# A graph attention layer on one core: the head and the second round of the pipeline put in another order

## The chip, the core and the metric

The kernel runs on one core of a Trainium2 chip. The metric is the device time of one execution in microseconds (us). Five engines run their own instruction streams beside each other and wait for one another by semaphores: PE (matrix products), DVE and ACT (vector and scalar work), POOL (vector work, slower) and SP (which only issues DMAs here).

## What is computed

There are 128 graphs of 64 nodes with 384 features each; `adj` (128 x 64 x 64) is 0 or 1 here. With every bias random and small:

```python
h = jnp.maximum(_layernorm(x, axis=-1), 0.0)
adj = dep_type_matrix != 0
dep_emb = dep_emb_table[dep_type_matrix]
hi_t = einsum('bid,de->bie', h, W1_w[:HID])[:, :, None, :] + einsum('bijd,de->bije', dep_emb, W1_w[HID:]) + W1_b
hj_t = einsum('bjd,de->bje', h, W2_w[:HID])[:, None, :, :] + einsum('bijd,de->bije', dep_emb, W2_w[HID:]) + W2_b
relevance = jnp.sum(hi_t * hj_t, axis=-1)
A = softmax(where(adj, relevance, NEG), axis=2)
h_syn = relu(einsum('bij,bjd->bid', A, h) @ gcn_w + gcn_b)
x = x + h_syn @ Wo_w + Wo_b
```

Where an edge exists its type is 1, so the type's part of both factors is one vector each: q (from W2) and p (from W1), each the embedding row times the 64 lower rows of the weight, plus its bias. Relevance is then h M h' plus a term by row, a term by column and a constant, with M = W1 W2' (384 x 384). The kernel tests at run time whether a type above 1 occurs (`has_types`) and jumps over a slower branch when, as here, none does.

## The kernel before

**Tiles.** A supertile is 8 graphs, 512 rows of x, in KT = 4 tiles of 128 rows; there are 16 supertiles. h stands transposed in hT, in DC = 3 chunks of 128 features. Products keep fp32 accuracy by splitting each operand in a high and a low fp16 part (`..._hi`, `..._lo`) and adding three fp16 products; those are the lines L1142 to L1144 whatever the product is (`split_product`).

**A supertile's work on PE**, in five kinds: `g_chunk` (G = M h, three chunks of 9 matmuls with 512 columns), `hg_tile` (h times gcn_w, four tiles of 9 matmuls with 385 columns, the 385th is the row term), `transposed_attention` and `aggregation` (attention times h gcn_w), `scores_of` (h' G, 48 short matmuls) and `output` (four tiles of 9 matmuls with 384 columns). ACT takes the high part of every result out of its bank (`g_high_part`, `hg_high_part`, `z_parts`), DVE the low part (`g_low_part`, `hg_low` inside `rows_and_low`, `z_low_part`), and both of them do the softmax between them: `masked_scores` and the maximum on DVE, `move_scores` and `exponentials` on ACT, `attention` on DVE.

**The order** is written out by hand, one list for each engine; semaphores tie the lists together. Supertiles 0 and 1 are handled apart from the rest. First comes a head: W1 and W2 are transposed on PE (L1163) and copied to SBUF, M is made in three chunks (L1183), p and q are projected (L1202), a bound on M's size fixes M's power-of-two scale (`scale`, by `peak_exponent`, `scale_from_exponent`, `scale_ready`), the norms of gcn_w and Wo fix theirs, x(0) is normalised (`first_coefficients`, `early_normalise`) and its h is transposed on PE (L1175) rather than by DMA. Then the first round (`g_chunk` and `hg_tile` of supertile 0), the jump on `has_types` (L256), the transposes of h(1), the scores of 0, and the second round: supertile 1 with attention and output of 0. From supertile 2 on h is transposed by DMA, and the loop has two supertiles in each pass.

**POOL** adds the output bias to x (`add_bias`, L408), turns adj from int to the score bias (`make_bias`, L402, two halves), works out the layer norm coefficients of later supertiles (`coefficients`, L345, 20 short instructions) and takes the low part of h (L432). **SP** issues the loads, `transpose_h` and the stores.

The 8 banks of PSUM are handed from product to product: `FIRST_HG_BANK` gives the banks of the four hg tiles of supertile 0, `EARLY_BANK` those of the transposes of h.

Of the kernel before, what the change touches and what calls it, by code (L numbers as in the profile page):

```python
# [5 lines left out]
def gnn_layer_program(nc, x, adj, emb, W1, b1, W2, b2, gcn_w, gcn_b, Wo, bo, out):  # L6
# [50 lines left out]
    with ctx:  # L57
# [136 lines left out]
        EARLY_BANK = (3, 4, 5)  # L194
        FIRST_HG_BANK = (3, 4, 5, 0)
        WARM_UP = 10
        EARLY_WIDE = 2
# [8 lines left out]
        early_bank = [bank[b][:, :].rearrange("p (k t) -> p k t", k=KT) for b in EARLY_BANK]  # L206
# [53 lines left out]
        def _(sp):  # L260
# [64 lines left out]
        def _(pool):  # L325
# [53 lines left out]
            def main_coefficients(s):  # L379

                pool.wait_ge(stats_ready, s + 1)

                if isinstance(s, int) and s <= 3:
                    pool.wait_ge(coef_ready, COEF_STEPS * s)
                    pool.wait_ge(h_ready, 2 * KT * min(s, 2))
                else:
                    pool.wait_ge(h_ready, 2 * KT * s)
                coefficients(s, third_stats6 if isinstance(s, int) and s == 2 else stats6, *normal_terms(s), coef_ready)

            pool.dma_start(bo_all[:, 0, :], bo.partition_broadcast(P)).then_inc(bo_loaded, 16)  # L390
# [52 lines left out]
            token_low(2, range(0, HALF_TILES))  # L443
            token_low(2, range(HALF_TILES, KT))
# [9 lines left out]
        def _(act):  # L454
# [39 lines left out]
            def early_high_part(s, c):  # L494
                act.wait_ge(early_t, DC * s + c + 1)
                nc.scalar.activation(hT_parts[s][:, :, 0, c, :], early_bank[c], ACT.Relu).then_inc(early_high, 1)
# [77 lines left out]
            early_high_part(0, 1)  # L574
            early_high_part(0, 2)
# [12 lines left out]
            types_above(2)  # L588
            g_high_part(0, 2)
            g_whole(2)  # L590
            hg_high_part(0, 0)
            types_above(3)
            hg_high_part(0, 1)
            early_normalise(1, range(0, EARLY_WIDE))
# [20 lines left out]
            def move_scores(s):  # L615
                act.wait_ge(s_done, s + 1)
                for g in range(GT):
# [24 lines left out]
            def second_round():  # L642
                for c in range(DC):
                    early_high_part(1, c)
                for c in range(DC):
                    wo_high_part(c)
                move_scores(0)
                g_high_part(1, 0)
                g_whole(0)
                exponentials(0)  # L650
                g_high_part(1, 1)
                g_whole(1)
                third_tokens(range(0, HALF_TILES))
                attention_out(1)
                g_high_part(1, 2)
                g_whole(2)
                third_tokens(range(HALF_TILES, KT))
                aggregated(1)
# [29 lines left out]
        def _(dve):  # L688
# [26 lines left out]
            def early_low_part(s, c):  # L715
                dve.wait_ge(early_high, DC * s + c + 1)
                nc.vector.scalar_tensor_tensor(hT_parts[s][:, :, 1, c, :], early_bank[c], 0.0, hT_parts[s][:, :, 0, c, :],
# [6 lines left out]
            def first_coefficients():  # L724
# [7 lines left out]
                dve.wait_ge(q_copied, 2)  # L732
                nc.vector.tensor_reduce(pq_size[:, :], pq_cols[:, :].unsqueeze(2), AX.X, ALU.max,
                                        apply_absolute_value=True).then_inc(top_step, 1)
                dve.wait_ge(coef_step, 1)
                nc.vector.scalar_tensor_tensor(sq, gap, D / 4, gap, ALU.mult, ALU.mult).then_inc(coef_step, 1)
                dve.wait_ge(top_step, 3)
                nc.vector.tensor_tensor(pq_size[:, :], pq_size[:, :], w_top[:, :, :].rearrange("p n c -> p (n c)"),
                                        ALU.max).then_inc(top_step, 1)
                dve.wait_ge(coef_step, 4)  # L740
                nc.vector.scalar_tensor_tensor(var, sq, D * EPS, var, ALU.add, ALU.add).then_inc(coef_step, 1)
                dve.wait_ge(top_step, 4)
                nc.vector.tensor_tensor(w_bound[:, :], pq_size[:, 0:DC], pq_size[:, DC:2 * DC],
                                        ALU.mult).then_inc(top_step, 1)
# [3 lines left out]
                dve.wait_ge(top_step, 5)  # L748
                nc.vector.tensor_reduce(bound_sum[:, :], w_bound[:, :], AX.X, ALU.add).then_inc(bound_ready, 1)
# [9 lines left out]
                def refine(n):  # L759
# [4 lines left out]
                times_var(0)  # L764
                refine(0)
                square(1)
                times_var(1)
                refine(1)
                square(2)
                dve.wait_ge(bound_wide, 1)  # L770
                nc.vector.tensor_scalar(peak[:, SC_M:SC_M + 1], pq_bank[:, BOUND, 0:1], TINY, None,
                                        ALU.max).then_inc(scale_step, 1)
                times_var(2)
                peak_exponent(SC_M, SC_M + 1, 1)
                refine(2)
                scale_from_exponent(SC_M, SC_M + 1, 1)
                dve.wait_ge(coef_step, 15)
                nc.vector.tensor_scalar(ln_mul, root, H_SCALE * D ** 0.5, None, ALU.mult).then_inc(coef_step, 1)
                scale_ready(SC_M, SC_M + 1, 1, m_scale_ready)
                dve.wait_ge(coef_step, 16)  # L780
                nc.vector.scalar_tensor_tensor(ln_add, total, -0.5, ln_mul, ALU.mult, ALU.mult)\
                  .then_inc(coef_ready, COEF_STEPS)
# [718 lines left out]
```

## Time and profile before

| | us |
|---|---|
| median of 3 runs | 365.49 (364.24 to 365.90) |
| the profiled execution's own time | 364.34 |
| its span | 362.4 |
| around the span | 1.94 |
| PE busy | 350.7, 97% of the span |
| ACT busy | 271.6, 75% |
| DVE busy | 262.4, 72% |
| POOL busy | 172.8, 48% |

The span runs from the first to the last instruction of the profiled execution, and every start below is counted from its beginning. TensorE's granted clock was full throughout. A matmul's end is modelled: in a row of back-to-back matmuls with 385 columns each shows 0.33 us, though they start 0.16 us apart. An idle time in brackets is counted from the modelled end, so the next matmul's start moved by 0.16 us more than the bracket says.

### The profile page before, as it was taken

What the parts mean: (1) busy time and instruction counts of PE and PEld (TensorE: products, weight loads), DVE (VectorE), ACT (ScalarE), POOL (GpSimd) and SP (SyncE); (2) the same over time, 40 slices, a digit from 0 to 9 for tenths busy, and PEclk for the clock granted to TensorE, in tenths of its full rate; (3) what the DMA queues carried; (4) which work ended last, traced back from release to release, by engine and by line L of the source; (5) the groups of instructions that cost most, each with busy time, mean ns of one, the idle gap of its engine ahead of it and who ended that gap; (6) DMA issues with size and microseconds to landing.
All of it is one profiled execution on the core that took longest, in us unless ns stands there. A gap on an engine that the chain in (4) does not pass through costs nothing.

```text
span 362.4 us, 9435 instructions
## 1 busy us (share of the span) xinstructions
PE 350.7 (97%) x3124; PEld 217.7 (60%) x3124; DVE 262.4 (72%) x668; ACT 271.6 (75%) x577; POOL 172.8 (48%) x349
## 2 busy tenths in 40 slices
PE   7998879999999999999999999999999999999986
PEld 7764546565756566565756666565756656565753
DVE  0998698594968767695867767695867768576664
ACT  3398795978698877778698877778788777765732
POOL 2056735655627183745728183744718174670000
DMA  7993608955547393655548393655648363544053
GB/s 220 325 251 90 175 5 140 225 132 153 145 134 207 87 260 88 196 110 151 151 127 221 87 258 89 185 114 142 167 113 234 87 174 87 117 92 143 2 143 121
DMA packets 82215, 53.87 MB, mean 149 GB/s; under 512 B 45666, under 2 KB 82148, under 8 KB 82196
## 3 DMA queue, kind: packets, MB, share of 16 engines
q1 hardware_dynamic: 81488, 53.22, 56.6%
q0 software_dynamic: 64, 0.20, 0.3%
q10 hardware_dynamic: 644, 0.20, 0.2%
q8 instruction: 11, 0.18, 0.2%
q14 instruction: 8, 0.07, 0.1%
HBM read 17.44 MB, written 12.58 MB: 83 GB/s over the span
## 4 chain that ended last, share of the span: by engine, by line
PE 85%; DVE 7%; ACT 2%; DMA 2%; POOL 2%; issue 2%; DVEq 0%; SPq 0%; ACTq 0%; POOLq 0%
PE bank L1142 24%; PE bank L1143 23%; PE bank L1144 23%; PE bank L1242 3%; PE bank L1393 3%; PE bank L1388 3%; PE bank L1250 2%; DMA x_all<-in_L_gnn_W_w_dram 2%; DVE stats L711 1%; PE bank L1359 1%; ACT h_tok L491 1%; PE bank L1175 1%; POOL root_sq L345 1%; PE bank L1458 1%; PE bank L1460 1%
## 5 line engine op out<-in xcount | busy, mean ns | idle before, releaser
L432 POOL TENSOR_TENSOR h_parts<-h_tok,h_parts 128x1536 f16<-128x1536 f32 (+1 forms) x15 | 43.8, 2922 | 101.2 <-ACT h_parts L473 93.6
L1142 PE MATMUL bank<-gw_hi,hT 128*128 128x385 f16 x192 | 63.0, 328 | 2.2 <-DVE hg_lo L812 2.2
L1144 PE MATMUL bank<-gw_hi,hT 128*128 128x385 f16 x192 | 62.7, 327 | 0.0
L408 POOL TENSOR_TENSOR x_all<-x_all,bo_all 128x1536 f32 (+1 forms) x16 | 54.9, 3439 | 16.0 <-ACT h_tok L491 16.0
L1143 PE MATMUL bank<-gw_lo,hT 128*128 128x385 f16 x192 | 62.5, 326 | 0.0
L1142 PE MATMUL bank<-wo_hi,z_hi 128*128 128x384 f16 x180 | 58.8, 327 | 0.0
L1143 PE MATMUL bank<-wo_lo,z_hi 128*128 128x384 f16 x180 | 58.7, 326 | 0.0
L1144 PE MATMUL bank<-wo_hi,z_lo 128*128 128x384 f16 x180 | 58.7, 326 | 0.0
L1142 PE MATMUL bank<-hT,m_hi 128*128 128x512 f16 x144 | 54.6, 379 | 0.0
L1143 PE MATMUL bank<-hT,m_hi 128*128 128x512 f16 x144 | 54.6, 379 | 0.0
L1144 PE MATMUL bank<-hT,m_lo 128*128 128x512 f16 x144 | 54.6, 379 | 0.0
L895 DVE TENSOR_TENSOR g_parts<-bank,g_parts 128x512 f16<-128x512 f32 x48 | 33.2, 691 | 28.3 <-ACT bank L546 27.9
L541 ACT ACTIVATE g_parts<-bank,pair_bias 128x512 f16<-128x512 f32 x48 | 32.9, 685 | 18.3 <-PE bank L1144 18.3
L553 ACT ACTIVATE z_hi<-bank,gcn_bias 128x512 f16<-128x512 f32 x48 | 33.8, 704 | 12.0 <-PE bank L1393 12.0
L1018 DVE TENSOR_TENSOR z_lo<-bank,z_hi 128x512 f16<-128x512 f32 x48 | 32.9, 685 | 8.5 <-ACT bank L555 8.4
L560 ACT ACTIVATE hg_hi<-bank 128x384 f16<-128x384 f32 x64 | 32.6, 511 | 8.5 <-PE bank L1144 8.5
L1026 DVE SCALAR_TENSOR_TENSOR x_all<-bank,out_scale,x_all 128x384 f32 (+1 forms) x64 | 36.3, 610 | 1.2 <-PE bank L1464 1.1
L473 ACT ACTIVATE h_tok<-x_all,ln_add,ln_mul 128x384 f32 (+1 forms) x52 | 36.5, 703 | 0.3
L473 ACT ACTIVATE h_parts<-x_all,ln_add,ln_mul 128x384 f16 (+1 forms) x52 | 36.4, 699 | 0.0
L812 DVE SCALAR_TENSOR_TENSOR hg_lo<-bank,hg_hi 128x384 f16<-128x384 f32 x64 | 35.2, 550 | 0.0
L555 ACT ACTIVATE bank<-bank,gcn_bias 128x512 f32<-128x512 f32 x48 | 32.7, 680 | 0.0
L546 ACT ACTIVATE bank<-bank,pair_bias 128x512 f32<-128x512 f32 x48 | 31.5, 655 | 0.0
(163 smaller groups left out, 658.5 us busy)
## 6 DMA issues: line engine op xcount, KB each, us to landing
x_all<-in_x_dram SPq DMA_DIRECT2D x16, 768.0 KB, 6.1
out_dram<-x_all SPq DMA_DIRECT2D x15, 768.0 KB, 4.5
hg_parts<-hg_lo SPq DMA_DIRECT2D x32, 192.0 KB, 3.4
hg_parts<-hg_hi SPq DMA_DIRECT2D x32, 192.0 KB, 3.9
x_all<-in_L_gnn_W_w_dram SPq DMA_DIRECT2D x2, 576.0 KB, 5.2
out_dram<-x_all SPq DMA_DIRECT2D x4, 192.0 KB, 1.9
gcn_raw<-in_L_gnn_gcn_w_dram SPq DMA_DIRECT2D x1, 576.0 KB, 11.0
x_all<-in_L_gnn_Wo_w_dram SPq DMA_DIRECT2D x1, 576.0 KB, 11.6
```

Source lines behind the costliest of these rows:

```text
L408: nc.gpsimd.tensor_tensor(x_all[:, s, :, :], x_all[:, s, :, :], bo_all[:, :, :].broadcast_to([P, KT, D]), ALU.add).then_inc(x_biased, 1)
L432: ins = nc.gpsimd.tensor_tensor(h_parts[:, at, 1, :], h_tok[:, at, :], h_parts[:, at, 0, :], ALU.subtract)
L473: nc.scalar.activation(to, x_all[:, s, k, :], ACT.Relu, bias=ln_add[:, k:k + 1], scale=ln_mul[:, k:k + 1]).then_inc(h_ready, 1)
L541: nc.scalar.activation(g_parts[:, c, :, 0, :], g_bank[c], ACT.Identity, bias=pair_bias[:, c:c + 1], scale=PROJ).then_inc(g_high, 1)
L553: nc.scalar.activation(z_hi[:, c, :], z_bank, ACT.Relu, bias=gcn_bias[:, c:c + 1], scale=Z_DOWN).then_inc(z_high, 1)
L812: nc.vector.scalar_tensor_tensor(hg_lo[:, k, :], bank[hg_banks(s)[k]][:, 0:D], PROJ, hg_hi[:, k, :], ALU.mult, ALU.subtract).then_inc(hg_s ...
L895: nc.vector.tensor_tensor(g_parts[:, c, :, 1, :], g_bank[c], g_parts[:, c, :, 0, :], ALU.subtract).then_inc(g_split, 1)
L1018: nc.vector.tensor_tensor(z_lo[:, c, :], z_bank, z_hi[:, c, :], ALU.subtract).then_inc(z_split, 1)
L1026: nc.vector.scalar_tensor_tensor(x_all[:, s, k, :], bank[O_BANK[k]][:, 0:D], out_scale[:, 0:1], x_all[:, s, k, :], ALU.mult, ALU.add).then ...
L1142: nc.tensor.matmul(dst, lh, rh, start=(c == 0), stop=False)
L1143: nc.tensor.matmul(dst, lh, rl, start=False, stop=False)
L1144: last = nc.tensor.matmul(dst, ll, rh, start=False, stop=(c == DC - 1))
```

## The change

The head and the second round are written in another order, and some work changes its engine.

- W2's three transposed chunks are copied by ACT, where DVE did it.
- q and p are projected before M. M has q as a 385th column in all three chunks, so the first part of the pair vector comes with M; the six matmuls that made it (12 passes of fp32) are gone, and DVE copies three columns instead (`q_row`). The third pair row and the sum of p q go into the first g chunk.
- On DVE M's scale is worked out amid x(0)'s coefficients, which now come after the bound and after the four statistics. DVE normalises 3 tiles of x(0) and ACT 1 (2 and 2 before).
- The norms' transposes and their broadcast move behind the transposes of h(0) and behind the first g chunk.
- The test for types runs after hg tile 1 in place of tile 2, and hg(0,3) has bank 7 in place of bank 0. The transposes of h(1) have banks 1, 2 and 3.
- On POOL the bias load waits for W2's data, the first half of the adjacency's bias comes before the coefficients of supertile 1, the second before those of 2, and the four fp16 copies of h(2) are made by POOL, where DVE made them.
- SP loads the adjacency's second half before x(2), behind it before.
- In the second round PE has hg(1,0) and hg(1,1) ahead of the transposed attention, and hg(1,3) behind scores(1). ACT and DVE follow with another order of their own.

The diff, cut to what the prediction speaks of:

```diff
-        EARLY_BANK = (3, 4, 5)
-        FIRST_HG_BANK = (3, 4, 5, 0)
+        EARLY_BANK = ((3, 4, 5), (1, 2, 3))
+        FIRST_HG_BANK = (3, 4, 5, 7)
...
             sp.dma_start(adj_all[:, 0:HALF, :], adj_rows[:, 0:HALF, :]).then_inc(adj_loaded, 16)
+            sp.dma_start(adj_all[:, HALF:, :], adj_rows[:, HALF:, :]).then_inc(adj_rest_loaded, 16)
             sp.wait_ge(x_loaded, 16)
             load_x(2)
-            sp.dma_start(adj_all[:, HALF:, :], adj_rows[:, HALF:, :]).then_inc(adj_rest_loaded, 16)
...
             add_bias(0)
+            make_bias(0)
             main_coefficients(1)
             pool.wait_ge(h_ready, 2 * KT * 2)
-            make_bias(0)
+            make_bias(1)
             main_coefficients(2)
-            make_bias(1)
...
+            def third_high_part(k):
+
+                pool.wait_ge(third_token, k + 1)
+                nc.gpsimd.tensor_copy(h_parts[:, k, 0, :], h_tok[:, k, :]).then_inc(h_ready, 2)
...
+            for c in range(DC):
+                act.wait_ge(w_transposed, DC + c + 1)
+                nc.scalar.activation(w2T[:, c, 0:D], bank[DC + c][:, 0:D], ACT.Copy).then_inc(w2_copied, 1)
             gcn_norm()
+            m_high_part(0)
+            m_high_part(1)
             wo_norm()
-            m_high_part(0)
-            early_normalise(0, range(EARLY_WIDE, KT))
-            m_high_part(1)
-            early_high_part(0, 0)
+            early_normalise(0, range(FIRST_WIDE, KT))
             m_high_part(2)
...
             dve.wait_ge(w_copied, DC)
             nc.vector.tensor_reduce(w_top[:, 1, :], w1T, AX.X, ALU.max, apply_absolute_value=True).then_inc(top_step, 1)
+            dve.wait_ge(pq_projected, 1)
+            nc.vector.tensor_copy(w2T[:, :, D], pq_bank[:, 0:DC, 0]).then_inc(q_copied, 1)
+            nc.vector.tensor_copy(pq_cols[:, 0:DC], pq_bank[:, 0:DC, 0]).then_inc(q_copied, 1)
             dve.wait_ge(w2_copied, DC)
...
+            dve.wait_ge(pq_projected, 2)
+            nc.vector.tensor_copy(pq_cols[:, DC:2 * DC], pair_bank[:, 0:DC, 0]).then_inc(q_copied, 1)
+            bound_of_product()
+            part_statistics(0, range(KT))
             first_coefficients()
...
+            statistics(2)
+            dve.wait_ge(type_row, 1)
+            nc.vector.tensor_reduce(type_top[:, :], bank[6][0:1, 0:4], AX.X, ALU.max).then_inc(type_step, 1)
...
+            def m_chunk(d):
+                for c in range(DC):
+                    last = nc.tensor.matmul(bank[d][:, 0:D + 1], w1T[:, c, d * P:(d + 1) * P], w2T[:, c, :],
+                                            start=(c == 0), stop=(c == DC - 1))
+                last.then_inc(m_done, 1)
...
+            pe.wait_ge(q_copied, 1)
+            m_chunk(0)
             pe.wait_ge(bound_ready, 1)
...
-            for e in range(DC - 1):
-                for c in range(DC):
-                    nc.tensor.matmul(pair_bank[:, DC + 1 + e, :], w1T[:, c, e * P:(e + 1) * P],
-                                     spread(pq_cols[:, c:c + 1]), start=(c == 0), stop=(c == DC - 1))
...
             for k in range(KT):
-                if k == DC:
-
-                    pe.wait_ge(g_split, 1)
                 hg_tile(0, k, 0, gcn_ready if k == 0 else None)
-                if k == 2:
+                if k == 1:
...
                 free_hg_tile(1, 0, 1)
+                free_hg_tile(1, 1, 1)
                 transposed_attention(1)
-                free_hg_tile(1, 1, 1)
+                free_hg_tile(1, 2, 1)
                 aggregation(1, Z_BANK)
-                for k in range(2, KT):
-                    free_hg_tile(1, k, 1)
                 scored_supertile(1, 1)
+                free_hg_tile(1, 3, 1)
                 pe.wait_ge(wo_split, DC)
                 output(1)
```

PE in the head, before, from the transposes of the weights (`bank<-ident,x_all`) to the first matmul of the first round; `bank<-x_all` is M and `bank<-e_col,x_all` the projection of p and q:

```order
L1163 MATMUL bank<-ident,x_all 128x128 x18
L1183 MATMUL bank<-x_all 128x384 x4
L1202 MATMUL bank<-e_col,x_all 128x64 x6
L1183 MATMUL bank<-x_all 128x384 x2
L1183 MATMUL bank<-x_all 128x385 x3
L1212 MATMUL bank<-bound_sum,ones 128x64
L1217 MATMUL bank<-pq_cols,x_all 128x64 x6
L1222 MATMUL bank<-ident,norm_part 1x128 x2
L1188 MATMUL bank<-pq_cols,x_all 128x64 x3
L1175 MATMUL bank<-ident,h_tok 128x128 x12
L1227 MATMUL bank<-norm_top,ones 128x2
```

The same place now:

```order
L1184 MATMUL bank<-ident,x_all 128x128 x18
L1208 MATMUL bank<-e_col,x_all 128x64 x6
L1214 MATMUL bank<-x_all 128x385 x3
L1233 MATMUL bank<-bound_sum,ones 128x64
L1214 MATMUL bank<-x_all 128x385 x6
L1220 MATMUL bank<-pq_cols,x_all 128x64 x6
L1198 MATMUL bank<-ident,h_tok 128x128 x12
L1244 MATMUL bank<-ident,norm_part 1x128 x2
L1163 MATMUL bank<-hT,m_hi 128x512
L1164 MATMUL bank<-hT,m_hi 128x512
L1165 MATMUL bank<-hT,m_lo 128x512
L1220 MATMUL bank<-pq_cols,x_all 128x64 x3
```

The projection has moved ahead of all of M, the six matmuls of L1217 are gone, and the norms (`ident,norm_part`) stand behind the transposes of h (`ident,h_tok`), with three pair rows inside the first chunk.

POOL between the output bias (`x_all<-x_all,bo_all`), the halves of the adjacency (`adj_all<-adj_all`) and the first coefficients; some lines only changed their number:

```order
-L408 TENSOR_TENSOR x_all<-x_all,bo_all 128x1536
+L410 TENSOR_TENSOR x_all<-x_all,bo_all 128x1536
+L404 TENSOR_SCALAR adj_all<-adj_all 128x2048
 L345 TENSOR_TENSOR root_sq<-stats 128x4
 L345 TENSOR_TENSOR half_sum<-stats 128x4
```

The first half of the adjacency's conversion has moved ahead of supertile 1's coefficients.

ACT in the second round, from the transposes' high parts (`hT<-bank`) to the exponentials (L628), before:

```order
L496 ACTIVATE hT<-bank 128x4x128 x3
L513 ACTIVATE wo_hi<-x_all,scale 128x384 x3
L622 ACTIVATE score_moved<-bank 64x256 x2
L541 ACTIVATE g_parts<-bank,pair_bias 128x8x64
L546 ACTIVATE bank<-bank,pair_bias 128x512
L628 ACTIVATE bank,row_sum<-bank,exp_bias,exp_scale 128x64 x4
```

and now (L640 are the exponentials):

```order
L522 ACTIVATE wo_hi<-x_all,scale 128x384
L505 ACTIVATE hT<-bank 128x4x128 x3
L634 ACTIVATE score_moved<-bank 64x256
L522 ACTIVATE wo_hi<-x_all,scale 128x384 x2
L550 ACTIVATE g_parts<-bank,pair_bias 128x8x64
L634 ACTIVATE score_moved<-bank 64x256
L555 ACTIVATE bank<-bank,pair_bias 128x512
L550 ACTIVATE g_parts<-bank,pair_bias 128x8x64
L555 ACTIVATE bank<-bank,pair_bias 128x512
L640 ACTIVATE bank,row_sum<-bank,exp_bias,exp_scale 128x64 x4
```

The move of the scores is cut in two with three other instructions between its halves, and the exponentials stand behind two g chunks rather than one.

## Rows read from the trace of the kernel before

**Rows 1.** Windows, one stretch: PE, PEld, DVE, ACT, POOL (us, instructions), PEclk, DMA, GB/s

```profile
60.00:80.48 20.48, 20.48 (x189) 12.48 (x188) 14.99 (x38) 17.67 (x38) 11.41 (x24) 1.00 0.75 177
```

**Rows 2.** Timeline of PE, 8 to 29 us: start, duration, instruction, [idle before]

```profile
8.89 2.82 PE L1183 MATMUL bank<-x_all 128*128 128x384 f32 x8
11.55 1.45 PE L1202 MATMUL bank<-e_col,x_all 65*128 65x64 f32 x12
...
16.30 1.50 PE L1217 MATMUL bank<-pq_cols,x_all 128*128 128x64 f32 x12
...
19.20 1.53 PE L1175 MATMUL bank<-ident,h_tok 128*128 128x128 f32 x12 [0.56 <-ACT h_tok L491]
...
22.58 0.38 PE L1142 MATMUL bank<-hT,m_hi 128*128 128x512 f16 x1
...
28.41 0.33 PE L1142 MATMUL bank<-gw_hi,hT 128*128 128x385 f16 x1
```

**Rows 3.** Timeline of DVE, 8 to 28 us

```profile
10.85 1.34 DVE L822 TENSOR_REDUCE w_top<-x_all 128x3 f32<-128x1152 f32 x1
...
17.28 0.16 DVE L781 SCALAR_TENSOR_TENSOR ln_add<-first_sum,ln_mul 128x4 f32<-128x4 f32 x1
...
22.31 0.15 DVE L861 TENSOR_SCALAR peak<-bank 128x2 f32<-128x2 f32 x1
...
24.47 0.21 DVE L875 TENSOR_SCALAR gcn_bias<-gcn_raw,scale 128x3 f32<-128x3 f32 x1
...
27.39 0.23 DVE L805 SCALAR_TENSOR_TENSOR gw_lo<-pair_all,scale,gw_hi 128x3 f16<-128x3 f32 x1
```

**Rows 4.** Timeline of ACT, 22 to 30 us

```profile
22.93 1.16 ACT L507 ACTIVATE x_all<-adj_all,const_all 128x1024 f32<-128x1024 int32 x1
...
29.08 1.15 ACT L507 ACTIVATE x_all<-adj_all,const_all 128x1024 f32<-128x1024 int32 x1 [0.29 <-DMA adj_all<-in_adj_dram]
```

**Rows 5.** Timeline of POOL, 34 to 52 us

```profile
34.64 1.90 POOL L402 TENSOR_SCALAR adj_all<-adj_all 128x2048 f32<-128x2048 int32 x1 [2.43 <-ACT h_tok L491]
...
51.58 3.54 POOL L432 TENSOR_TENSOR h_parts<-h_tok,h_parts 128x768 f16<-128x768 f32 x2 [7.59 <-DVE h_parts L1076]
```

**Rows 6.** All instructions of L1033: ns min/median/max, first and last start

```profile
L1033 DVE TENSOR_SCALAR masks<-adj_all,row_term x64: 243/250/1061, 39.0 to 344.2; 128x64 f32 x48, 128x64 f32<-128x64 f32 x16
```

**Rows 7.** Timeline of DVE at 323 us

```profile
323.20 1.55 DVE L1033 TENSOR_SCALAR masks<-adj_all,row_term 128x64 f32<-128x64 f32 x4
```

**Rows 8.** Timeline of POOL, 315 to 326 us

```profile
313.98 10.23 POOL L408 TENSOR_TENSOR x_all<-x_all,bo_all 128x1536 f32<-128x1536 f32 x3
```

**Rows 9.** Timeline of PE, 34 to 40 us

```profile
34.48 0.33 PE L1144 MATMUL bank<-gw_hi,hT 128*128 128x385 f16 x1
35.90 1.50 PE L1175 MATMUL bank<-ident,h_tok 128*128 128x128 f32 x12 [1.09 <-DVE hg_lo L812]
...
39.67 0.22 PE L1250 MATMUL bank<-hT,g_parts 128*64 128x64 f16 x2 [1.10 <-issue]
39.82 0.39 PE L1142 MATMUL bank<-hT,m_hi 128*128 128x512 f16 x1
```

**Rows 10.** PE's sequencer on L256, the jump on has_types: ns min/median/max, start

```profile
L256 PEldq TENSOR_LOAD <-has_types x1: 488/488/488, 34.5 to 34.5; - x1
...
L256 PEldq COMPARE_BRANCH  x1: 350/350/350, 35.4 to 35.4; - x1
```

**Rows 11.** Timeline of DVE, 34 to 68 us

```profile
34.34 0.13 DVE L919 TENSOR_SCALAR has_types<-type_top 1x1 int32<-1x1 f32 x1
...
37.19 1.89 DVE L717 SCALAR_TENSOR_TENSOR hT<-bank,hT 128x512 f16<-128x512 f32 x3 [0.96 <-ACT hT L496]
...
67.66 0.69 DVE L895 TENSOR_TENSOR g_parts<-bank,g_parts 128x512 f16<-128x512 f32 x1 [3.28 <-ACT bank L546]
```

**Rows 12.** Timeline of PE, second round and the round behind it

```profile
54.20 0.34 PE L1142 MATMUL bank<-gw_hi,hT 128*128 128x385 f16 x1 [2.18 <-DVE hg_lo L812]
...
68.89 0.33 PE L1142 MATMUL bank<-gw_hi,hT 128*128 128x385 f16 x1
```

More of the change, by code:

```diff
@@ L763, in first_coefficients @@
                 square(0)
[L764 to L776, printed above, removed]
+                scale_ready(SC_M, SC_M + 1, 1, m_scale_ready)
+                for n in range(3):
+                    if n:
+                        square(n)
+                    times_var(n)
+                    refine(n)
                 dve.wait_ge(coef_step, 15)
                 nc.vector.tensor_scalar(ln_mul, root, H_SCALE * D ** 0.5, None, ALU.mult).then_inc(coef_step, 1)
-                scale_ready(SC_M, SC_M + 1, 1, m_scale_ready)
                 dve.wait_ge(coef_step, 16)
@@ L872, in _ @@
             scale_ready(SC_WO, SC_GCN + 1, 5, scale_step)
-            part_statistics(1, range(1, 2))
             dve.wait_ge(scale_step, 9)
@@ L913, in _ @@
             dve.wait_ge(pair_bias_made, 3)
-            rows_and_low(0, 0)
-            dve.wait_ge(type_row, 1)
-            nc.vector.tensor_reduce(type_top[:, :], bank[7][0:1, 0:4], AX.X, ALU.max).then_inc(type_step, 1)
-            rows_and_low(0, 1)
-            dve.wait_ge(type_step, 1)
-            nc.vector.tensor_scalar(has_types[0:1, :], type_top[0:1, 0:1], 0.0, None, ALU.is_gt).then_inc(types_known, 1)
-            rows_and_low(0, 2)
-            rows_and_low(0, DC)
+            for k in range(KT):
+                rows_and_low(0, k)
             with typed(dve):
@@ L1180, in spread, with projected @@
                 return column.broadcast_to([column.shape[0], SPREAD])
-            def m_step(d, c, columns):
-                return nc.tensor.matmul(bank[d][:, 0:columns], w1T[:, c, d * P:(d + 1) * P], w2T[:, c, 0:columns],
-                                        start=(c == 0), stop=(c == DC - 1))
+            def projected(to, dep):
+                for c in range(DC):
+                    last = nc.tensor.matmul(to[:, c, :], dep[:, c * P:(c + 1) * P], spread(e_col[:, :]), start=True,
+                                            stop=True)
+                last.then_inc(pq_projected, 1)
+            def m_chunk(d):
+                for c in range(DC):
+                    last = nc.tensor.matmul(bank[d][:, 0:D + 1], w1T[:, c, d * P:(d + 1) * P], w2T[:, c, :],
+                                            start=(c == 0), stop=(c == DC - 1))
+                last.then_inc(m_done, 1)
             def pair_row(e):
@@ L1280, in hg_tile @@
                               lambda d: (gw_hi[:, d, :], gw_lo[:, d, :]), before).then_inc(hg_done, 1)
-            for c in range(DC):
-                g_chunk(c, 0, chunk_ready(0) if c == 0 else None)
+            g_chunk(0, 0, chunk_ready(0))
+            pe.wait_ge(norms_top, 1)
+            nc.tensor.matmul(bank[6][:, NORM_WIDE], ones[0:1, :], norm_top[0:1, :], start=True,
+                             stop=True).then_inc(norms_wide, 1)
+            g_chunk(1, 0)
+            g_chunk(2, 0)
             for k in range(KT):
-                if k == DC:
-                    pe.wait_ge(g_split, 1)
                 hg_tile(0, k, 0, gcn_ready if k == 0 else None)
-                if k == 2:
+                if k == 1:
                     pe.wait_ge(type_sums, 4)
-                    pe.wait_ge(pairs_copied, 2)
-                    nc.tensor.matmul(bank[7][0:1, 0:4], ones[:, 0:1], type_sum[:, :], start=True,
+                    pe.wait_ge(pairs_copied, DC + 1)
+                    nc.tensor.matmul(bank[6][0:1, 0:4], ones[:, 0:1], type_sum[:, :], start=True,
                                      stop=True).then_inc(type_row, 1)
```

201 lines of the change are left out of this document (104 added, 97 removed).

## The prediction, made before the changed kernel ran

> **What bounds the kernel now.** I read the windows first. A steady round of one supertile takes 20.48 us, and PE is busy for all of it, while ACT has 17.67 and DVE 14.99 [rows 1]. The change touches nothing in those rounds, so time can come or go only in the head, in the first two rounds, and where the second round hands over to the third. There I read PE's timeline, since PE's starts give the sum directly. The points I follow are the first g chunk (22.58) and the first hg tile of supertile 0 (28.41) [rows 2], the first g chunk of supertile 1 (39.82) [rows 9], and the first hg tile of supertile 2 (68.89) [rows 12]. Between them stand the only idle times that the change can take away: 1.09 us ahead of the transposes of h(1), 1.10 us inside the scores of supertile 0, for which the profile names no releaser ("issue") [rows 9], and 2.18 us ahead of hg(1,3) [rows 12]. Counted by starts each is about 0.16 us more, since a matmul's shown end lies 0.16 us behind the point at which the next one may start: the transposes came 1.42 us after the last hg matmul (34.48 to 35.90), where 0.16 is the normal distance, so 1.26 is lost.
>
> **Step 1, the head up to the first g chunk: -1.0.** M now needs q. The projection ran at 11.55 without an idle time before it [rows 2], so the embedding rows had landed by then. They cannot be used before the transposes of the weights end, at 8.89. I take a landing at 10.0, near the middle. Then q is in its column at about 10.9. PE does 18 passes of M at 2.82/8 = 0.353 us [rows 2], which is 6.35, one broadcast of 0.25, and 12 pair passes at 1.50/12 = 0.125, which is 1.5: PE is free for the transposes at 19.0. DVE does the second weight maximum, 1.34 [rows 3], some seven short instructions of the bound (about 1.0), four statistics (about 1.95) and then coefficients and M's scale together (about 2.9): ln_add comes at about 18.0, where it was 17.28 [rows 3]. With 3 tiles of x(0) in place of 2 DVE is done at 19.3, ACT with its single tile earlier, and the transposes start at 19.4, against 19.20 [rows 2]. Before, 3.38 us passed from there to the first g chunk, because PE had six pair passes twice, the norms' broadcast and the sum of p q to do. Now only the two norm rows stand there, and the chunk waits for chunk 0's transposes (0.5), its high part (0.6) and its low part (0.6): 21.6 in place of 22.58. The removed W2 copies and the removed pair passes (1.50, rows 2) are in this -1.0, not beside it. If the rows land at 9.0 the step is -1.9, though most of it is then lost in step 2, and if they land at 11.5 it is +0.4.
>
> **Step 2, up to the first hg tile: +1.7.** Inside the g chunks PE now has the third pair row and the sum (8 passes, 1.0) and the norms' broadcast (0.15): it would reach hg(0,0) at 21.6 + 5.83 + 1.15 = 28.6. But gcn_w's scale now waits for the broadcast behind the first chunk, at 21.6 + 1.94 + 1.0 = 24.55. From that peak to gcn_bias it was 22.31 to 24.68 with two statistics and a low part between; without these I take 1.3, so 25.85, and from gcn_bias to the last low part of gcn_w 24.68 to 27.62, 2.94 [rows 3]. hg(0,0) starts at 29.1 with the handing over, +0.7. The other 1.0 is a new collision. The first adjacency half (1.90 us on POOL, rows 5) stood at 34.64. Now it runs as soon as ACT's first two counts of types are done: the second of these ended at 24.1 [rows 4], about 23.9 now, so it covers 23.9 to 25.8, exactly the scale's short instructions on DVE, which read and write SBUF. What that does is seen once in this trace: of 64 masks of 250 ns one took 1061 [rows 6]; it is in the group of four that began at 323.20 and took 1.55 us [rows 7], while POOL's long addition ran until 324.21 [rows 8]. The first mask ended just when POOL's instruction did. I take it that the chain is held likewise, until 25.8: +1.0, with 0 and 1.9 (the whole instruction) as bounds. Sum of the step: 28.41 becomes 30.1.
>
> The Trainium skill ("SBUF — State Buffer", section "Who interferes with whom") says that DVE and GpSimd share one pair of ports as an exclusive lock, that copies and tensor_scalar in a two-port mode take it, and that whoever issues first keeps it for the whole instruction. The late mask agrees with it. By that page the scale's 128x2 instructions would block as the mask did, and the sum stays as it is; without it 1.0 us would go.
>
> **Step 3, from hg(0,0) to g_chunk(1,0): -2.0.** Before, has_types was written at 34.34 [rows 11], PE's sequencer loaded it from 34.5 and finished the jump at 35.75 [rows 10], and the transposes came at 35.90. Now the test follows hg tile 1: has_types is known some 1.6 us before PE's last hg matmul, and load plus jump take 1.25, under queued matmuls. The bank of hg(0,3) no longer makes PE wait either. I take the whole 1.26 as gone (bounds 0 and 1.26), and 0.2 around the type sum with it. The 1.10 inside the scores comes two matmuls before their end; I read it as code that arrives late after the jump, and with the jump 1.5 us earlier against the matmuls it should be hidden: 1.18 by starts (bounds 0 and 1.18). What is late next is the low part of h(1): its three instructions took 1.89 behind ACT's [rows 11], and one of Wo's parts now stands ahead of ACT's high parts. I take a wait of 0.6 (bounds 0 and 1.2). Sum -1.26 - 0.2 - 1.18 + 0.6 = -2.0.
>
> The Trainium skill ("Runtime: NRT & Kernel Launch", section "Instruction fetch mechanics") says that a taken branch to code outside the fetched window stalls the engine until the page is there. No row names the 1.10 so; by that rule an earlier jump hides it, as I take it, unless the target now falls otherwise against a page's edge, and then it stays.
>
> So g_chunk(1,0) starts at 39.82 + 1.7 - 2.0 = 39.5: -0.3.
>
> **Step 4, the second round: 0.0.** The 2.18 ahead of hg(1,3) goes, 2.34 by starts, as hg(1,3) now follows the scores. Its place is taken by shorter waits, which I estimate from the order and the trace's durations: 0.2 for g parts ahead of the attention, 0.7 for hg(1,0)'s low part and 0.6 for z's, 1.5 in all. Output of 0 would start 0.8 us nearer. But the first hg tile of supertile 2 shares its banks with g(2,0), whose low part ended at 68.27 with PE there at 68.89 [rows 11, 12]: 0.6 us of slack. The chain in front of that (scores of 1, exponentials, normalising x(3), g(2,0)) has the same ACT work as before, and it starts no earlier, because ACT now takes three hg parts in a row behind z. I therefore put hg(2,0) at the same distance from g_chunk(1,0) as before. Bounds: -0.8 if ACT's chain does come earlier, +0.5 if it slips.
>
> **Edits that I cost at nothing.** x(2) behind the adjacency's second half: the half had landed by 29.08 with x(2) ahead of it [rows 4], so both are there by about 29.1 in either order, and DVE's statistics of x(2), now behind g(0,1)'s low part, run from about 30.5. The bias of Wo, which waits for W2, is needed only at about 19.3. POOL's four fp16 copies of h(2): by 1.90 for 2048 elements and by 3.54/2 for 768 [rows 5] one of 384 costs between 0.36 and 0.88 us; I take 0.5. ACT's tokens come earlier than before, and the transposing DMA behind them has about 2 us to spare, which would be gone at 1.0 a copy.
>
> **Sum.** -1.0 + 1.7 - 2.0 + 0.0 plus rounding: -0.3 us against the profiled execution's 364.34 (span 362.4 and 1.94 around it), so 364.0. That execution lies 1.15 below the median of the runs shown, so I apply the difference to the median: 365.49 - 0.3 = 365.2. I call no change what is within 0.5%, 1.8 us, about what a measurement can tell here.
>
> **Rivals.**
> - *POOL doesn't block short instructions.* Only a 128x64 mask is seen held, and 128x2 ones may pass. Then hg(0,0) is at 29.1 and the sum -1.3: 364.2. If also step 4 keeps its 0.8: -2.1, 363.4.
> - *The jump is not hidden* (slower). If PE's sequencer reads has_types only when its queued matmuls are nearly over, or the late code stays late, both stalls of step 3 remain: -0.3 + 2.44 - 0.6 = +1.5, 367.0. It decides from the point where load, jump and fetch together need more than the 1.6 us that the earlier test gives. For it: the load before came within 0.1 us of the write, so it was a wait on the value and nothing proves that it can overlap. Against it: a sequencer that can queue matmuls has no reason to wait for their end.
> - *POOL too slow with the copies of h(2).* At 1.5 us each, far beyond both bounds, four add 6.0 in place of 2.0, and the transposed h(2) comes 2 us late for g_chunk(2,0): 367.2. A row of POOL held by DVE's own SBUF work could bring that.
>
> **How the numbers follow.** Forecast as summed 0.42; no block 0.22; no block and step 4 gains 0.08; jump not hidden 0.18; POOL late 0.10. Faster by over 0.5% comes from the third case and the early end of the second: 0.15. Slower by over 0.5% comes from the last and from half of the fourth: 0.19. Within: 0.66. The range goes from 363.3 (the fast cases) to 367.4 (jump or POOL late).
>
> **What would show it.** First g chunk of 0 at about 21.6 and hg(0,0) at about 30.1, with one of DVE's 128x2 scale instructions near 1 us long and ending with POOL's adjacency row: step 2 right; hg(0,0) at 29.1 with all of them under 0.2 us: no block. No idle time ahead of the transposes of h(1) and none by "issue" in the scores: step 3. g_chunk(1,0) at 39.5, an hg(2,0) that waits for g(2,0)'s low part, and the span 362.1. A wait of the g chunks of supertile 2 for the DMA of h(2) would make it slower, and an unhidden jump at 36 to 38 us would too.

## The result and the profile after: slower by 0.3%

The changed kernel took 365.82 us in the median of 22 runs against 364.97 for the kernel before, ratio 1.0031 (95% interval 1.0015 to 1.0046). Forecast was -0.3 us. The medians lie 0.85 us apart, the ratio makes it +1.1: the time lies in the range, but the sign was wrong. The profiled execution has a span of 363.5 us (before 362.4) and an own time of 365.29.

The windows of the changed kernel's trace show at once what was not in my sum (columns as in [rows 1]):

```profile
10.00:11.50 1.50, 1.29 (x12) 1.30 (x12) 0.38 (x3) 0.00 (x0) 0.00 (x0) 1.00 1.07 345
11.50:12.00 0.50, 0.50 (x4) 0.48 (x4) 0.50 (x1) 0.00 (x0) 0.00 (x0) 0.65 1.10 384
12.00:13.00 1.00, 1.00 (x3) 0.42 (x2) 0.96 (x6) 0.53 (x1) 0.00 (x0) 0.50 1.05 376
...
14.00:15.00 1.00, 1.00 (x3) 0.48 (x2) 1.00 (x3) 0.00 (x0) 0.00 (x0) 0.50 1.06 373
15.00:15.40 0.40, 0.40 (x4) 0.27 (x3) 0.37 (x2) 0.00 (x0) 0.00 (x0) 0.92 1.09 361
```

The granted clock, the third number from the end, is 0.50, the 1.2 GHz level, from about 11.7 to 15.1 us, at the very start of M. PE's timeline, to be read against [rows 2, 9, 12]:

```profile
7.54 1.20 PE L1184 MATMUL bank<-ident,x_all 128*128 128x128 f32 x9 [1.16 <-DMA x_all<-in_L_gnn_W_w_dram]
10.21 1.55 PE L1208 MATMUL bank<-e_col,x_all 65*128 65x64 f32 x12 [1.46 <-DMA x_all<-in_L_gnn_W_b_dram]
11.59 3.85 PE L1214 MATMUL bank<-x_all 128*128 128x385 f32 x6
...
15.45 4.11 PE L1214 MATMUL bank<-x_all 128*128 128x385 f32 x12
...
20.67 1.48 PE L1198 MATMUL bank<-ident,h_tok 128*128 128x128 f32 x12
...
22.78 0.38 PE L1163 MATMUL bank<-hT,m_hi 128*128 128x512 f16 x1 [0.41 <-DVE hT L737]
...
31.44 0.32 PE L1163 MATMUL bank<-gw_hi,hT 128*128 128x385 f16 x1 [1.42 <-DVE gw_lo L827]
...
37.56 1.47 PE L1198 MATMUL bank<-ident,h_tok 128*128 128x128 f32 x12
...
40.93 0.39 PE L1163 MATMUL bank<-hT,m_hi 128*128 128x512 f16 x1 [0.70 <-DVE hT L737]
...
54.84 0.34 PE L1163 MATMUL bank<-gw_hi,hT 128*128 128x385 f16 x1 [0.54 <-DVE hg_lo L834]
57.02 0.32 PE L1163 MATMUL bank<-wo_hi,z_hi 128*128 128x384 f16 x1 [0.54 <-DVE z_lo L1039]
...
69.94 0.34 PE L1163 MATMUL bank<-gw_hi,hT 128*128 128x385 f16 x1 [0.86 <-DVE g_parts L918]
```

The first six passes of M take 3.7 us by starts; the twelve behind them, nearly all at the full clock, 3.9. PE had waited 1.16 us for W2 and 1.46 us for the embedding rows just before. The starts, side by side:

| start of | before | forecast | after |
|---|---|---|---|
| first g chunk of 0 | 22.58 | 21.6 | 22.78 |
| first hg tile of 0 | 28.41 | 30.1 | 31.44 |
| first g chunk of 1 | 39.82 | 39.5 | 40.93 |
| first hg tile of 2 | 68.89 | 68.6 | 69.94 |
| span | 362.4 | 362.1 | 363.5 |

DVE's chain for gcn_w's scale, and POOL's instruction beside it ([rows 3, 5] before):

```profile
18.21 0.16 DVE L787 SCALAR_TENSOR_TENSOR ln_add<-first_sum,ln_mul 128x4 f32<-128x4 f32 x1
...
26.07 0.16 DVE L887 TENSOR_SCALAR peak<-bank 128x2 f32<-128x2 f32 x1 [0.86 <-PE bank L1303]
26.26 0.89 DVE L810 TENSOR_SCALAR peak_bits<-peak 128x2 int32<-128x2 int32 x1
...
27.66 0.23 DVE L898 TENSOR_SCALAR gcn_bias<-gcn_raw,scale 128x3 f32<-128x3 f32 x1
27.80 1.47 DVE L731 BATCH_NORM_STATS2 stats<-x_all 128x6 f32<-128x384 f32 x3
...
31.06 0.23 DVE L827 SCALAR_TENSOR_TENSOR gw_lo<-pair_all,scale,gw_hi 128x3 f16<-128x3 f32 x1
```

```profile
25.23 1.90 POOL L404 TENSOR_SCALAR adj_all<-adj_all 128x2048 f32<-128x2048 int32 x1 [1.67 <-ACT x_all L516]
```

peak_bits, an instruction on two elements in each partition, takes 0.89 us and ends at 27.15, with POOL's at 27.13. The instruction before it, which reads PSUM, ran in 0.16 us while POOL's was already under way.

The single profile does not carry the whole result. Every run has its span and its mean clock, and these fall in groups. At full clock (0.998 or more) the changed kernel has a mean span of 362.8 us (5 of 22 runs); at 0.994 or 0.995, which fits one low stretch, 363.7 (13); at 0.991, which fits two, 365.5 (4). The kernel before has 362.2 (45 of the 77 runs made beside the experiments) and 363.8 with one low stretch (32), and never two. So the full-clock runs of the two kernels are 0.7 us apart, and all runs together 1.0 (363.8 against 362.8).

### The profile page after: what moved, and what is told of

It reads as the page before. It is cut to its first block, busy times and chain, and to the rows that moved or that the text cites. A ratio compares the mean times of both kernels' runs of the same rounds, so it can differ in the third digit from the quotient of the medians.

```text
span 363.5 us, 9409 instructions
## 1 busy us (share of the span) xinstructions
PE 350.3 (96%) x3112; PEld 216.2 (59%) x3112; DVE 261.9 (72%) x665; ACT 272.3 (75%) x579; POOL 174.9 (48%) x353
## 4 chain that ended last, share of the span: by engine, by line
PE 84%; DVE 5%; ACT 5%; DMA 2%; issue 1%; POOL 1%; ACTq 1%; DVEq 0%; POOLq 0%
PE bank L1163 23%; PE bank L1164 23%; PE bank L1165 23%; PE bank L1413 3%; PE bank L1408 3%; PE bank L1259 3%; PE bank L1214 2%; DMA x_all<-in_L_gnn_W_b_dram 2%; PE bank L1267 2%; PE bank L1379 1%; ACT bank L640 1%; ACT h_tok L482 1%; ACT hg_hi L569 1%; PE bank L1475 1%; PE bank L1477 1%
## 5 line engine op out<-in xcount | busy, mean ns | idle before, releaser
L1047 DVE SCALAR_TENSOR_TENSOR x_all<-bank,out_scale,x_all 128x384 f32 (+1 forms) x64 | 36.3, 609 | 1.2 <-PE bank L1481 1.1
```

What stands on the lines that cost most here:

```text
L1047: nc.vector.scalar_tensor_tensor(x_all[:, s, k, :], bank[O_BANK[k]][:, 0:D], out_scale[:, 0:1], x_all[:, s, k, :], ALU.mult, ALU.add).then ...
```

## The experiments

Ratios are to the kernel before, run on the same chip in turn. Lines are those of each kernel's own text.

**a_fill: PE kept busy while it waits.**

```diff
+                if n:
+                    keep_warm(2, 7)
                 pe.wait_ge(loaded, 16)
...
+            keep_warm(3, 7)
             pe.wait_ge(dep_loaded, 16 * 4)
```

> The changed kernel with five more warm-up matmuls on ones (results unused), two while PE waits for W2's rows and three while it waits for the embedding rows. Theory 1 (clock): PE's idle time of 1.16 and 1.46 us ahead of the projection is what precedes the fall of the granted clock to 0.5 at 11.7 us. Filled, the clock stays at 1.00, six passes of M take 2.1 us in place of 3.7, the first g chunk starts at 21.9 in place of 22.78, the first hg tile at 30.6 in place of 31.44, and the span is 362.6 in place of 363.5. Theory 2 (late data): the head is late because q and the coefficients are late, and the slow passes of M are hidden beside DVE. Then the clock may come back but the first g chunk stays at 22.7 to 22.8 and the span at 363.4.

Ratio 1.0029 (1.0008 to 1.0049). PE's timeline, then the two instructions that met:

```profile
11.75 2.16 PE L1216 MATMUL bank<-x_all 128*128 128x385 f32 x6
...
22.11 0.38 PE L1163 MATMUL bank<-hT,m_hi 128*128 128x512 f16 x1 [0.41 <-DVE hT L737]
...
31.76 0.32 PE L1163 MATMUL bank<-gw_hi,hT 128*128 128x385 f16 x1 [2.41 <-DVE gw_lo L827]
```

```profile
25.87 1.87 DVE L817 TENSOR_SCALAR unscale<-peak_bits 128x2 f32<-128x2 f32 x1
```

```profile
25.82 1.90 POOL L404 TENSOR_SCALAR adj_all<-adj_all 128x2048 f32<-128x2048 int32 x1 [2.33 <-ACT x_all L516]
```

```profile
31.00:32.00 1.00, 0.24 (x2) 0.21 (x3) 1.00 (x4) 1.00 (x3) 0.98 (x5) 1.00 0.70 229
...
33.00:34.00 1.00, 1.00 (x5) 0.48 (x4) 1.00 (x4) 1.00 (x3) 0.91 (x4) 0.50 0.35 131
```

The head did what theory 1 says: the clock stayed, six passes took 2.0, the g chunk came 0.67 earlier. The span did not follow. DVE's scale chain now met POOL's instruction at its start and was held for 1.87 us, PE waited 2.41, and in the profiled execution the clock fell behind that wait instead. In 9 of 12 runs the clock was full, and still their median span was 363.5, 0.7 above the changed kernel's own full-clock runs. So the clock is one cause and POOL's hold another.

POOL's instruction met the chain so fully because it came later, at 25.82 in place of 25.23, though the head was earlier. It waits for ACT's counts of types, and these waited for the adjacency:

```profile
23.36 1.15 ACT L516 ACTIVATE x_all<-adj_all,const_all 128x1024 f32<-128x1024 int32 x1 [1.14 <-DMA adj_all<-in_adj_dram]
```

The profiles of all six changed kernels with added warm-up matmuls (a_fill, c_fill_bias, d_stats, h_dep, k_late_six, m_early_six) have that wait, of 0.52 to 1.14 us, and those of the four without them (the changed kernel, b_bias, g_round, e_late) have none. Three of these four reached the counts later, with a slow head; but in e_late, whose head was at full clock, ACT began them at 21.96 without a wait. No run shows why.

**b_bias: POOL's half back behind the coefficients.**

```diff
             add_bias(0)
-            make_bias(0)
             main_coefficients(1)
             pool.wait_ge(h_ready, 2 * KT * 2)
+            make_bias(0)
             make_bias(1)
```

> The changed kernel with POOL's first adjacency half behind the coefficients of supertile 1, as it was before. Theory (POOL holds DVE): the instruction peak_bits (0.89 us in the changed kernel) takes 0.15, gcn_bias and the first hg tile come 0.75 earlier against the first g chunk (8.66 becomes 7.9), and the span is 362.8 in place of 363.5. Rival (it was the wait for the norms' broadcast, or what stands behind gcn_bias on DVE): peak_bits may be short, but the first hg tile comes less than 0.2 us earlier.

```profile
26.39 0.17 DVE L810 TENSOR_SCALAR peak_bits<-peak 128x2 int32<-128x2 int32 x1
```

```profile
30.84 0.32 PE L1163 MATMUL bank<-gw_hi,hT 128*128 128x385 f16 x1 [0.70 <-DVE gw_lo L827]
```

From the first g chunk (22.91) to hg(0,0) it is 7.93, against 8.66: 0.73 gained, as expected, and the profiled span is 362.9. At full clock the span is 362.1 (3 runs), 0.7 under the changed kernel's. But 9 of 12 runs lost the clock once or twice, so the ratio was 1.0022 (0.9998 to 1.0046).

**c_fill_bias: both edits.**

> The changed kernel with both edits together: the five warm-up matmuls of a_fill and POOL's adjacency half behind the coefficients, as in b_bias. Theory (two causes: clock, then POOL holding DVE, whose wait also drops the clock a second time): the first g chunk at 22.1, the first hg tile at 29.9 in place of 31.44, no wait of PE above 1 us from 12 to 60 us, the clock at 1.00 in nearly all runs, span 361.9 in place of 363.5, ratio to before about 0.999. Rival (each gain is given back by the next wait, as in a_fill): the span of full-clock runs stays at 362.1 or above, as in b_bias.

```profile
30.10 0.32 PE L1163 MATMUL bank<-gw_hi,hT 128*128 128x385 f16 x1 [0.70 <-DVE gw_lo L827]
```

Ratio 0.998 (0.9962 to 0.9998), full clock in 11 of 12 runs, span 362.2; the first g chunk came at 22.16, and PE's longest wait from there to 60 us was 0.70. The two causes together are the whole loss and a little more. The rival was right in one thing: the full-clock span is no better than b_bias's 362.1.

**d_stats: one statistic moved into DVE's idle time.**

```diff
-            part_statistics(1, range(0, 1))
+            part_statistics(1, range(0, 2))
...
-            part_statistics(1, range(1, KT))
+            part_statistics(1, range(2, KT))
```

> c_fill_bias with one more statistic of x(1) ahead of the norms' broadcast, where DVE idles 0.86 us, in place of behind gcn_bias. Theory (three statistics behind gcn_bias hold gcn_w's low parts): from gcn_bias to the last low part of gcn_w 0.45 us less, first hg tile 0.4 earlier than in c_fill_bias, span 361.5. Rival (ACT's high parts of gcn_w, 1.63 us behind gcn_bias, set the low parts): no change against c_fill_bias, within 0.1.

```profile
29.65 0.32 PE L1163 MATMUL bank<-gw_hi,hT 128*128 128x385 f16 x1 [0.24 <-DVE gw_lo L827]
33.02 0.19 PE L1316 MATMUL bank<-type_sum,ones 128*1 128x4 f32 x2 [0.25 <-ACT x_all L516]
```

hg(0,0) came 0.45 earlier than in c_fill_bias, so the statistics did hold the low parts. But 0.25 went to a new wait for ACT's counts of types, g_chunk(1,0) came only 0.13 earlier (39.47 against 39.60), and the span was 362.1, not 361.5. Ratio 0.9965 (0.9947 to 0.9983).

**h_dep: the embedding rows first on ACT's queue** (on top of d_stats).

```diff
-            act.wait_ge(e_one, 1)
-            act.dma_start(e_col[0:DE, :], emb[EDGE, :].rearrange("(k o) -> k o", o=1)).then_inc(e_loaded, 16)
             for W, b, dep in ((W2, b2, w2_dep), (W1, b1, w1_dep)):
...
+            act.wait_ge(e_one, 1)
+            act.dma_start(e_col[0:DE, :], emb[EDGE, :].rearrange("(k o) -> k o", o=1)).then_inc(e_loaded, 16)
```

> d_stats with the embedding rows loaded first on ACT's queue, the type's column behind them. If the order of issue sets when the rows land, the projection starts 0.5 earlier, at about 9.8, and with it the first g chunk (21.6) and the span (361.0 to 361.2). If the rows queue behind W2 and x(0) on the DMA engines, nothing moves: projection at 10.2 to 10.4, or it now waits for the column, and the span stays.

```profile
9.61 1.52 PE L1210 MATMUL bank<-e_col,x_all 65*128 65x64 f32 x12 [0.29 <-DMA e_col<-L_gnn_dep_emb_table_dram]
...
28.81 0.32 PE L1163 MATMUL bank<-gw_hi,hT 128*128 128x385 f16 x1 [0.24 <-DVE gw_lo L827]
```

The projection came 0.81 earlier than in d_stats, now waiting for the column, and all of it reached hg(0,0). Median 363.27, ratio 0.9958 (0.9941 to 0.9974), span 361.5 (361.0 to 361.2 was expected): the lowest of all versions, faster than the kernel before and, by the ratios, than the changed one.

**i_first: the projection first, in the kernel before.** Its six matmuls and their two waits go ahead of `m_step(0, ...)`.

> The kernel before with one part of the change alone: p and q are projected before M, all else as before. Theory 1 (clock): PE now idles from 8.8 to 10.2 for the embedding rows, the granted clock falls to 0.5 near 11.7 us for some 3 us as in the changed kernel, passes of M take 0.64 us, and the span rises from 362.4 by 1 to 2 us. Theory 2 (the clock falls for another reason, as the new order of M): the clock stays at 1.00, passes stay at 0.35, and the span rises by at most 0.7.

```profile
10.67 2.15 PE L1196 MATMUL bank<-e_col,x_all 65*128 65x64 f32 x12 [1.73 <-DMA x_all<-in_L_gnn_W_b_dram]
12.61 8.84 PE L1183 MATMUL bank<-x_all 128*128 128x384 f32 x18
```

Ratio 1.0088 (1.0054 to 1.0122). The wait, then the low clock (0.50 from about 11.4 to 18.3 us, twice as long as in the changed kernel), and 18 passes of M in 8.7 us. The order of M is not needed for it. The median span is 4.4 us above the full-clock spans of before, where I had expected 1 to 2. The one run at full clock has 364.2: by this single run 2.0 us is what the late projection costs by itself in the old order, and the rest is the clock. Part of that rest lies in the second round, where this profile loses the clock once more:

```profile
59.31 0.50 PE L1142 MATMUL bank<-gw_hi,hT 128*128 128x385 f16 x1 [2.13 <-DVE hg_lo L812]
```

```profile
60.00:62.00 2.00, 2.00 (x8) 0.97 (x7) 1.63 (x4) 0.23 (x1) 1.84 (x10) 0.50 0.21 43
```

**g_round: PE's old order in the second round.**

> The changed kernel with PE's order in the second round as before: hg(1,1) behind the transposed attention, hg(1,3) ahead of the scores. ACT and DVE keep the new order. Theory (the first hg tile of supertile 2 waits for g(2,0)'s low part, which hangs on ACT and DVE): a wait of 2 us or more comes back ahead of hg(1,2) or hg(1,3), the wait of 0.86 ahead of hg(2,0) goes or shrinks, and from g_chunk(1,0) to hg(2,0) it is 29.0 to 29.6 us, against 29.01, span within 0.5 us. Rival (PE's order gave what it looks like): the distance grows by 1 us or more, to 30 or beyond, and the span to 364.5.

```profile
PE bank L1163 <- DVE gw_lo L827: 1.4, 1, 1.4
PE bank L1379 <- DVE att_parts L1090: 1.1, 1, 1.1
...
PE bank L1163 <- DVE g_parts L918: 0.3, 1, 0.3
```

From g_chunk(1,0) at 41.15 to hg(2,0) at 69.98 it is 28.83, against 29.01 with the new order: PE's order there, with ACT and DVE in the new one, is worth nothing. No wait of 2 us came back, though; a wait of 1.1 moved to the attention, and I had its place wrong.

**e_late: the test for types behind hg tile 2 again.**

```diff
-                if k == 1:
+                if k == 2:
```

and DVE's two instructions between `rows_and_low(0, 0)` and `rows_and_low(0, 2)`, as before.

> The changed kernel with the test for types behind hg tile 2 again, on PE and on DVE, and bank 7 kept for hg(0,3). Theory (the early test hides load and jump): the transposes of h(1) start 1.0 to 1.3 later behind the last hg matmul (normally 0.16), the scores show a wait by issue again, and the first g chunk of supertile 1 comes 0.6 to 1.8 later against hg(0,0) (9.49 in the changed kernel), span 364.1 to 365.3. Rival (the freed bank hid the 1.26, not the test): both distances stay within 0.2 us.

```profile
39.05 1.50 PE L1200 MATMUL bank<-ident,h_tok 128*128 128x128 f32 x12 [2.12 <-issue]
```

From hg(0,0) at 30.64 to g_chunk(1,0) at 41.68 it is 11.04, against 9.49: +1.55, and the ratio is 1.0077 (1.0051 to 1.0103). The early test does hide the jump, and bank 7, which this kernel keeps, is not the reason. The wait was 2.12 and not the 1.0 to 1.3 that I expected, since has_types was only written at 37.5, when PE had no hg matmul left; in return the wait of 0.70 ahead of g_chunk(1,0) went. But no idle time by issue came back in the scores.

**k_late_six and m_early_six: where does the 1.10 in the scores come from?** Both have six warm-up matmuls, so that PE's program has the kernel before's length up to the scores; k has the late test too, m is else d_stats.

> The changed kernel with the late test of e_late and six warm-up matmuls (12 passes, three in each idle gap of the head), so that PE has as many instructions ahead of the scores as the kernel before. The late test alone (e_late) brought back the wait at the jump but not the 1.10 us by issue inside the scores. Theory (the 1.10 hangs on where in PE's program the scores stand, and shows when PE arrives right behind a jump): it comes back, 0.6 to 1.1 us, two or a few matmuls before the end of the scores. Rival (it hung on something else that the change took away, as the bank or ACT's order): no idle time by issue inside the scores, only the 2.1 us ahead of the transposes.

> d_stats with six warm-up matmuls in place of five, so that PE's program has as many instructions ahead of the scores as before, but with the early test. Theory (an early jump hides the late code, as I predicted): no idle time by issue in the scores, span 362.1 as in d_stats. Rival (place alone decides): an idle time of 0.6 to 1.1 us in the scores, of which the wait of 0.70 for h(1)'s low part hides part, span 362.2 to 362.6.

```profile
39.96 1.50 PE L1202 MATMUL bank<-ident,h_tok 128*128 128x128 f32 x12 [0.69 <-issue]
...
42.09 0.56 PE L1272 MATMUL bank<-hT,g_parts 128*64 128x64 f16 x23
43.18 0.19 PE L1272 MATMUL bank<-hT,g_parts 128*64 128x64 f16 x1 [0.52 <-issue]
```

In k it is back, 0.52 us one matmul before the scores' end, a little under the 0.6 to 1.1 expected; the wait ahead of the transposes was 0.69 and not 2.1. In m the 24 scores of that line run on without a gap (ratio 0.9975, 0.9958 to 0.9992; span 361.9). So it seems that both must meet: a place in the program's text and a jump just before. m also has d_stats's edits, so the test's place is not its only difference from k. That it is code arriving late fits both, but no row names it. k's ratio was 1.0078 (1.0049 to 1.0108).

**n_before_fill: the kernel before with its first gap filled.**

> The kernel before with two warm-up matmuls while PE waits for W2's rows (0.57 us idle). The kernel before too has executions at a mean clock of 0.995 (25 of 58 so far, span 363.6 to 364.0 against 362.2). If this gap is where its clock is lost, they become rare (under 2 in 10) and the median span is 362.2; if a later gap does it (the 1.1 and 2.2 us from 34 to 57), the share stays near 4 in 10.

```profile
54.00:55.00 1.00, 1.00 (x7) 0.59 (x6) 1.00 (x4) 0.79 (x2) 1.00 (x3) 0.98 0.00 0
55.00:56.00 1.00, 1.00 (x9) 0.55 (x7) 1.00 (x4) 0.00 (x1) 0.92 (x7) 0.50 0.08 16
```

6 of 10 runs still lost the clock (ratio 1.0007, 0.9986 to 1.0028), and this profile shows where: from 55 us, right behind the wait of 2.18 us ahead of hg(1,3). Filling the head's gap did not change the share, and i_first fell behind the same wait, so the kernel before most likely loses its clock in the second round, the changed one in the head. No execution of the kernel before with a fall was profiled.

This trace also bears on the place of the idle time by issue:

```profile
39.30 0.28 PE L1252 MATMUL bank<-hT,g_parts 128*64 128x64 f16 x6 [0.66 <-issue]
```

It stands six matmuls before the scores' end, where the kernel before [rows 9] and i_first, which has no matmul more or less ahead of the scores, have it two before. Two warm-up matmuls are four passes, and it moved by four matmuls. So its place seems fixed in PE's program, and its length is not: 1.10, 0.61 and 0.66.

## Why the prediction was wrong

The step that failed is **step 1, "the head up to the first g chunk: -1.0"**: it was +0.2. I priced M's passes at 0.353 us from [rows 2] and gave PE 1.1 us of waiting for the embedding rows (8.9 to 10.0) without asking what the wait does to the clock. In the profiled execution PE waited 1.16 and 1.46, and the next passes ran at half clock. e_late has the same instructions in its head; its profiled execution waited 0.48 and 1.35 and kept the clock:

```profile
11.62 2.16 PE L1216 MATMUL bank<-x_all 128*128 128x385 f32 x6
...
19.82 1.53 PE L1200 MATMUL bank<-ident,h_tok 128*128 128x128 f32 x12 [0.61 <-DVE h_tok L858]
...
21.98 0.38 PE L1165 MATMUL bank<-hT,m_hi 128*128 128x512 f16 x1 [0.41 <-DVE hT L737]
```

Its first g chunk is at 21.98, not 22.78: so the clock cost 0.8 of the 1.2. The other 0.4 is DVE's chain, which came later than I had summed: ln_add at 18.24 and not 18.0, DVE's three tiles of h done at 19.8 and not 19.3, and the transposes, which wait for them, at 19.82 and not 19.4.

Over all runs the clock is the smaller part of the loss: 17 of 22 runs have a low stretch, but so have 32 of 77 before, and 0.7 of the 1.0 us between the two kernels stands between their full-clock runs as well. The sign was wrong without the clock too.

The sum, as written, does not add up: -1.0 + 1.7 - 2.0 is -1.3. The +1.7 of step 2 is counted from the old start of hg(0,0) and has step 1's -1.0 in it. From the first g chunk step 2 is +2.7 (8.5 in place of 5.83), and -1.0 + 2.7 - 2.0 is the -0.3 that the starts (39.5 against 39.82) give as well.

**Step 2** ("+1.7", 8.5 us from the first g chunk to hg(0,0)) was 8.66. The collision with POOL is there, 0.73 us by b_bias where I took 1.0, and 1.87 in a_fill, inside my bounds of 0 and 1.9. I had missed the third statistic behind gcn_bias, 0.45 by d_stats. That the step came out so near is luck: the hold was 0.27 less than I took, and the statistic nearly made it up. The Trainium skill ("SBUF — State Buffer", section "Who interferes with whom") is borne out in both: two elements in each partition are enough to be held, until POOL's instruction ends. The rival "POOL doesn't block short instructions" is refuted.

**Step 3** ("-2.0", 9.4 us from hg(0,0) to g_chunk(1,0)) was 9.49. The waits of 1.26 and 1.18 went, 0.70 came for h(1)'s low part (0.6 forecast). e_late shows the reason for the first, and in the changed kernel has_types was written at 34.9 and the jump done at 36.3, under queued matmuls. The rival "the jump is not hidden" is refuted. The 1.18 went for another reason than mine, or for more than mine: in e_late it is gone too, with a late jump, and k_late_six, with six matmuls more, has 0.52 of it. So that term had the right size by luck.

**Step 4** ("0.0") was 29.01 in place of 29.07. The waits that replaced the 2.18 were 0.54 and 0.54 (the 0.7 for hg(1,0)'s low part did not come), and 0.86 at hg(2,0) gave the rest back; g_round confirms that PE's order moves nothing.

The sum of the profile: forecast -0.3, plus 0.8 for the clock, 0.4 for DVE's chain, 0.2 for step 2 and 0.1 for step 3, less 0.1 for step 4, is +1.1; without the clock's 0.8 it would be +0.3. The edits costed at nothing held: POOL's copies took 0.64 and 0.48 us each, and nothing waited for h(2) or x(2).

What stays open: why one and the same kernel keeps the clock in some runs and loses it in others, why 45 of 77 runs of before keep it, though the profiled one of them waited 2.18 us, what the idle time by issue is, and why the adjacency came later in a_fill than in e_late.

## What to carry to other kernels

When an edit makes PE wait early, price the matmuls behind the wait at both clock levels, and look at the clock of every run, not of the one profiled: here the groups of one kernel lie 0.9 to 2.7 us apart, more than most of the edits are worth. A short instruction on a critical chain needs a look at what POOL runs at that moment; and when one cure shows nothing, try it together with the next suspect before dropping it, as a_fill alone and b_bias alone brought next to nothing in the ratio (1.0029 and 1.0022, against 1.0031) and both together were faster than the kernel before. Filling a wait with matmuls whose results nobody uses gave the clock back. It cost nothing at full clock once POOL's half was out of the way (362.2 against b_bias's 362.1), and 0.7 us where it was not (363.5 against 362.8): look at the full-clock runs before and after such a cure.

## What the runs showed of the hardware

- The granted clock fell to 0.50 (the 1.2 GHz level) for about 3.4 us at a time: in the changed kernel after waits of 1.16 and 1.46 us near each other, in a_fill after 2.41, in n_before_fill after 2.18. In i_first it stayed there for about 6.8 us after 1.46 and 1.73. Like waits did not always bring it: e_late's profile (0.48 and 1.35 in the head, 2.12 at the jump) and the profile before (2.18) kept the full clock. Five warm-up matmuls in the first two gaps, together with b_bias's edit, took the share of runs with a fall from 17 in 22 to 1 in 12.
- A DVE instruction of two elements in each partition, from SBUF to SBUF, took 0.89 us in the changed kernel, 1.53 in k_late_six and 1.87 in a_fill beside one of POOL of 1.90, and ended within 0.03 us of it; in b_bias it took 0.17. One that reads PSUM took 0.16 us in the changed kernel, with POOL's under way.
- PE's sequencer read a flag and jumped over 1 us ahead of its matmuls: in the changed kernel the load began at 35.1 and the jump ended at 36.3, while the last hg matmul started at 37.4.
- An idle time of PE by issue, of 0.5 to 1.1 us, came in the scores only in kernels with the late test, and moved by four matmuls when four passes were put ahead of it (n_before_fill).
